# A decoder layer's self-attention with transposed scores and softmax sums from a column of ones, and the layer norms' epsilon added on POOL

## The chip, the cores and the metric

The kernel runs on one core of a Trainium2 chip. The metric is the device time of one execution in microseconds (us); smaller is better. Five engines work side by side, each through its own instructions in order, and wait for one another by semaphores: TensorE (PE; its weight loads are listed as PEld), VectorE (DVE), ScalarE (ACT), GpSimd (POOL) and SyncE (SP, which issues DMAs). PE's results lie in PSUM, which the code declares as eight banks of 128 partitions by 512 fp32 columns.

## The reference, cut to what matters

4096 tokens (64 sequences of 64) of width 128 pass through a self-attention, a cross-attention and a mixture of experts, each followed by a residual sum and a layer norm. The change lies in the self-attention (16 heads of 64, one shared key and value head) and in the layer norms of both attentions:

```python
def layernorm(x, g):
    mean = jnp.mean(x, axis=-1, keepdims=True)
    var = jnp.var(x, axis=-1, keepdims=True)
    return (x - mean) * jax.lax.rsqrt(var + EPS) * g
...
xn = layernorm(x, g1)
q = xn @ Wq.T
kv = xn @ Wkv.T
k, v = (kv[..., :DIM_HEAD], kv[..., DIM_HEAD:])
...
q, k = (l2norm(q), l2norm(k))
q, k = (q * srt, k * srt)
sim = jnp.einsum('bhid,bjd->bhij', q, k)
sim = jnp.where(causal_mask, max_neg, sim)
attn = jax.nn.softmax(sim.astype(jnp.float32), axis=-1).astype(sim.dtype)
out = jnp.einsum('bhij,bjd->bhid', attn, v)
out = out.transpose(0, 2, 1, 3).reshape(b, n, HEADS * DIM_HEAD)
out = out @ Wout.T
return layernorm(out, g2)
...
x = _layernorm(x + _L0_attn_ref(x, ...), axis=-1)
```

## The kernel before

The tokens are 32 tiles of 128 (two sequences each). The kernel first passes all tiles through the self-attention, then all through the cross-attention, then through the experts. Everything is written by hand: for each engine a function `body(i, p)` lists the stages of pass i, and `stage_of(fn, i, p, back)` calls a stage for tile i - back, so that one pass works on the layer norm of tile i + 2, the projections of tile i, the scores of i - 1, the values of i - 2, the output projection of i - 3 and the second norm of i - 4. Each engine goes through its stages in the order of that list; `wait_ge` on a semaphore holds the engine there. `pipeline` writes passes 0 to 7 out, runs the middle ones as a hardware loop of two passes, and writes the last ones out; the last stages of the last tiles run inside the first cross-attention passes (`cross(0)`, `cross(1)`).

A tile goes through the self-attention like this.

- DVE takes the statistics of a row (`ln_stats`, `ln_var`) and adds epsilon to the variance; POOL raises that to the power -0.5 (`ln_in`); DVE normalises (`ln_b`); PE transposes (`x_T`, line 1526); ACT and DVE split the result in two parts.
- PE multiplies by Wq in three passes for each 512 columns (lines 1515 to 1517, banks 2 and 3) and by Wkv (line 1539, bank 1).
- ACT squares (`squares`); DVE sums over each head (`sums`, line 974: 16 heads and the key, 17 sums from 1088 columns); POOL raises all 17 to the power -0.5 in one instruction (`norms`, line 534, tile `rq`); DVE caps them (`rinv`, line 981) and scales q out of PSUM in two halves (`qn`, line 987). PE can overwrite bank 2 or 3 with the next tile's q once its half is scaled.
- PE transposes q and k (lines 1548, 1554), adds the causal mask (line 1564) and multiplies (`scores`, line 1569): 32 products of 64 x 64 x 64, each recorded as two passes, for two sequences and two groups of heads, so that queries lie on partitions. ACT takes the exponential (`exp_half`).
- DVE sums over the keys (`softmax`, lines 1003 and 1005: `L`, `rL`); POOL multiplies the 1024 columns by the reciprocals (`weights`, line 539, tile `PR`).
- PE transposes the weights (`p_T`, line 1583), ACT copies them out (line 726), PE multiplies with a block-diagonal copy of v (`values`, line 1591; DVE and ACT write that copy, lines 997 and 710), ACT copies out (`o_T`, line 734), PE projects (`project`, line 1599).
- The second and third layer norm of the tile follow on DVE (`y_stats` to `tail_c`), with two more powers on POOL (`y_rstd`, line 544, and `z_rstd`, line 548).

In the profile `bank` is a PSUM bank, `arena` holds `wide`, `qn`, `OT` and Wout, `PT` the transposed weights, `VBD` the block-diagonal v.

Of the kernel before, what the change touches and what calls it, by code (L numbers as in the profile page):

```python
# [31 lines left out]
P = 128  # L32
# [16 lines left out]
def decoder(nc, x, ctxT, g1, wqT, wkvT, woutT, g2, xwq, xwk, xwvT, xwo, bo, wrT, br, wl1, bl1, wl2, bl2, bN, out, xbuf, zbuf):  # L49
# [24 lines left out]
    HVO = HEADS // NVO  # L74

    ctx = ExitStack()
    with ctx:
# [6 lines left out]
        bank = [ctx.enter_context(nc.psum_tensor(f"bank{i}", [P, 512], F32)) for i in range(8)]  # L84
# [6 lines left out]
        mhalf = sb("mhalf", [P, 32])  # L91
        euler = sb("euler", [P, 32])
# [12 lines left out]
        OT = arena[:, 2 * W:3 * W].rearrange("p (a q) -> p a q", a=NBLK)  # L105
# [30 lines left out]
        vS = sb("vS", [P, 2, DH])  # L136
# [13 lines left out]
        rL = sb("rL", [P, 2, HEADS])  # L150
        mx = sb("mx", [P, HEADS])
# [81 lines left out]
        zeroed, w_ids = sem("zeroed"), sem("w_ids")  # L233
# [11 lines left out]
        def staging(n):  # L245
# [11 lines left out]
            "pT_ps", "pT", "y", "r", "rb", "z1", "zrstd", "x2")}  # L257
# [14 lines left out]
        def pipeline(eng, body, first, last):  # L272


            for i in range(first):
                body(i, i % 2)
            with eng.Fori(first // 2, T // 2 - 1) as j:
                body(2 * j, 0)
                body(2 * j + 1, 1)
            for i in range(T - 2, last + 1):  # L280
                body(i, i % 2)
# [192 lines left out]
        def _(pool):  # L474
            def ln_in(t, p):
                pool.wait_ge(a["stats"], 3 * t + 3)
                nc.gpsimd.tensor_tensor(rs[:, p, :], ve[:, p, :], mhalf[:, 0:1], ALU.pow).then_inc(a["rstd"], 1)
# [6 lines left out]
            nc.gpsimd.memset(euler[:, :], 2.718281828459045).then_inc(consts, 1)  # L484
# [57 lines left out]
            def y_rstd(t, p):  # L542
                pool.wait_ge(a["y1"], 3 * t + 3)
                nc.gpsimd.tensor_tensor(rs2[:, :], ve2[:, :], mhalf[:, 0:1], ALU.pow).then_inc(a["yrstd"], 1)

            def z_rstd(t, p):
                pool.wait_ge(a["z1"], 3 * t + 3)
                nc.gpsimd.tensor_tensor(rs3[:, :], ve3[:, :], mhalf[:, 0:1], ALU.pow).then_inc(a["zrstd"], 1)  # L548
# [8 lines left out]
            def body(i, p):  # L557
# [3 lines left out]
                stage_of(norms, i, p, 0)  # L561
                stage_of(z_rstd, i, p, 4)
                stage_of(ln_in, i, p, -2)
                stage_of(y_rstd, i, p, 3)
                stage_of(weights, i, p, 1)
# [8 lines left out]
            def cross_tail(t, p):  # L574
                pool.wait_ge(b["z1"], 3 * t + 3)
                nc.gpsimd.tensor_tensor(rs3[:, :], ve3[:, :], mhalf[:, 0:1], ALU.pow).then_inc(b["zrstd"], 1)  # L576
# [81 lines left out]
        def _(act):  # L658

            def x_T(t, p):  # L660
                act.wait_ge(a["xT_ps"], t + 1)
                if later(t, 2):
                    act.wait_ge(a["q"], 2 * (t - 1))
                    act.wait_ge(a["xlo"], t - 1)
                nc.scalar.activation(xT[:, p, :], bank[first_x_bank(t)][:, 0:P], ACT.Copy, scale=g1_sb[:, 0:1])\
# [8 lines left out]
            def squares(t, p):  # L674
                if later(t, 1):
                    act.wait_ge(a["ssq"], t)
                for c in range(2):
                    act.wait_ge(a["q"], 2 * t + c + 1)
                    nc.scalar.activation(wide[:, c * HW:(c + 1) * HW], bank[2 + c][:, :], ACT.Square)\
                      .then_inc(a["sq"], 1)  # L680
                act.wait_ge(a["kv"], t + 1)
                nc.scalar.activation(wide[:, W:W + DH], bank[1][:, 0:DH], ACT.Square).then_inc(a["sq"], 1)
                if later(t, 2):
                    act.wait_ge(a["v0"], t - 1)
                    act.wait_ge(a["v1"], t - 1)
                nc.scalar.activation(vS[:, p, :], bank[1][:, DH:2 * DH], ACT.Copy).then_inc(a["vS"], 1)
# [1234 lines left out]
```

## Time and profile before

| what | before |
|---|---|
| time, median of 3 runs | 832.95 us (831.18 to 836.39) |
| the profiled execution | 833.86 us, its span 832.1 us |
| busy over the span | PE 770.5 us (93%), DVE 620.7 (75%), ACT 596.5 (72%), POOL 454.3 (55%) |
| self-attention | until some 330 us; cross-attention follows until some 690 us, then the experts |
| granted PE clock | 0.987 of full speed on the mean |

Times are from the start of the span. Busy shares are means over stages with different limits, and a busy PE is not PE at its peak, since its instructions overlap in the record. What bounds a stage is read from the waits and from the order in time within that stage.

### The profile page before, as it was taken

How to read it: one execution, taken by the hardware profiler on the slowest of the kernel's cores; microseconds unless marked ns; L12 is line 12 of the kernel's file. 1: busy time of each engine (PE TensorE's matmuls, PEld its weight loads, DVE VectorE, ACT ScalarE, POOL GpSimd, SP SyncE). 2: the span in 40 equal slices, each digit the busy share in tenths (PEclk: the TensorE clock that was granted, in tenths of full speed). 3: DMA queues.
4: the chain of work that ended last, by engine and by line, in shares of the span. 5: the costliest groups of instructions: out<-in, count | busy, mean ns of one | idle time of the engine just before them, and what ended most of it. 6: DMA issues, size and time to landing. Idle time of an engine off the chain costs nothing.

```text
span 832.1 us, 26529 instructions
## 1 busy us (share of the span) xinstructions
PE 770.5 (93%) x9276; PEld 646.4 (78%) x9308; DVE 620.7 (75%) x1834; ACT 596.5 (72%) x1444; POOL 454.3 (55%) x442
## 2 busy tenths in 40 slices
PE   3799999999999998899899999999999989989995
PEld 3577778777777877788788888887888878989962
DVE  3877878878877874789888888888888965744425
ACT  2688888878878874777778777676767667767735
POOL 6467776776777672222253535444443537776643
PEclk9899999999999999999999999999999989999998
DMA  8299999100000000000000000000000227878745
GB/s 273 67 159 165 162 161 156 16 0 0 0 0 0 0 3 2 6 7 7 7 22 17 23 17 20 20 20 20 16 23 14 72 76 225 254 221 250 248 157 210
DMA packets 69392, 64.79 MB, mean 78 GB/s; under 512 B 5702, under 2 KB 54985, under 8 KB 69168
## 3 DMA queue, kind: packets, MB, share of 16 engines
q1 hardware_dynamic: 62592, 51.42, 29.8%
q0 software_dynamic: 4624, 9.61, 3.3%
q10 hardware_dynamic: 2080, 2.49, 1.0%
q8 instruction: 59, 0.97, 0.5%
q14 instruction: 37, 0.30, 0.1%
HBM read 35.37 MB, written 28.58 MB: 77 GB/s over the span
## 4 chain that ended last, share of the span: by engine, by line
PE 47%; issue 19%; POOL 13%; DVE 9%; ACT 6%; DMA 3%; SPq 1%; POOLq 0%; DVEq 0%; ACTq 0%
PE bank L1715 7%; PE bank L1819 6%; PE bank L1515 5%; POOL rq L534 5%; PE bank L1517 5%; PE bank L1516 5%; POOL PR L539 3%; PE bank L1829 3%; PE bank L1703 3%; PE bank L1591 2%; PE bank L1599 2%; PE bank L1690 2%; ACT VBD L393 2%; DMA w_now<-in_wl 2%; POOL rs L548 1%
## 5 line engine op out<-in xcount | busy, mean ns | idle before, releaser
L393 ACT COPY VBD<-bank 64x512 f32<-64x512 f32 x192 | 111.4, 580 | 28.1 <-PE bank L1517 25.4
L571 POOL TENSOR_TENSOR PR<-PR,rL 128x1024 f32<-128x1024 f32 x32 | 60.9, 1904 | 107.9 <-DVE rL L1125 107.7
L534 POOL TENSOR_TENSOR rq<-ssq,mhalf 128x17 f32<-128x17 f32 x32 | 99.3, 3102 | 14.4 <-DVE ssq L974 13.8
L539 POOL TENSOR_TENSOR PR<-PR,rL 128x1024 f32<-128x1024 f32 x32 | 61.0, 1905 | 82.4 <-DVE rL L1005 82.4
L638 POOL DMA_INDIRECT zbuf<-arena x71 | 69.8, 983 | 31.6 <-issue 21.2
L626 POOL DMA_INDIRECT xbuf<-xg,slot x64 | 64.9, 1013 | 34.2 <-DVE xg L1320 21.6
L1819 PE MATMUL bank<-xT,w_now 128*128 128x128 f32 x568 | 77.3, 280 | 3.1 <-DMA w_now<-in_wl 2.7
L1819 PEld LDWEIGHTS bank<-xT,w_now 128*128 128x128 f32 x568 | 70.4, 195 | 4.6 <-issue 3.5
L1446 DVE SCALAR_TENSOR_TENSOR stage<-bank,b_now,early 128x128 f32<-128x128 f32 x142 | 43.3, 347 | 40.4 <-ACT early L892 32.6
L892 ACT ACTIVATE early<-bank,b_now 128x128 f32<-128x128 f32 x142 | 44.6, 365 | 35.8 <-PE bank L1819 35.7
L1715 PE MATMUL bank<-VBD,PT 128*64 128x128 f32 x1024 | 64.7, 280 | 3.2 <-ACT PT L808 3.2
L1715 PEld LDWEIGHTS bank<-VBD,PT 128*64 128x64 f32 x1024 | 56.8, 139 | 11.8 <-ACT PT L808 9.8
L1599 PE MATMUL bank<-arena 128*128 128x128 f32 x512 | 63.0, 276 | 1.1 <-ACT arena L734 0.7
L1591 PE MATMUL bank<-PT,VBD 128*128 128x512 f32 x128 | 63.4, 617 | 0.0
L808 ACT ACTIVATE PT<-bank 128x512 f32<-128x512 f32 x64 | 38.3, 600 | 34.7 <-PE bank L1703 34.0
L1599 PEld LDWEIGHTS bank<-arena 128*128 128x128 f32 x512 | 59.8, 192 | 2.3 <-ACT arena L734 1.6
L576 POOL TENSOR_TENSOR rs<-ve,mhalf 128x1 f32<-128x1 f32 x32 | 18.6, 581 | 70.5 <-DVE ve L1140 70.2
L1515 PE MATMUL bank<-vo_lo,cT_hi 96*128 96x512 f32 x128 | 54.8, 428 | 2.3 <-DVE VBD L393 1.5
L1112 DVE TENSOR_REDUCE mx<-bank 128x8 f32<-128x512 f32 x64 | 43.8, 684 | 17.3 <-PE bank L1690 17.0
L718 ACT ACTIVATE PR<-bank 128x512 f32<-128x512 f32 x64 | 34.7, 595 | 28.8 <-PE bank L1569 28.8
L1517 PE MATMUL bank<-vo_hi,cT_hi 96*128 96x512 f32 x128 | 50.4, 394 | 0.0
L1516 PE MATMUL bank<-vo_hi,cT_lo 96*128 96x512 f32 x128 | 50.4, 394 | 0.0
(253 smaller groups left out, 2296.0 us busy)
## 6 DMA issues: line engine op xcount, KB each, us to landing
w_now<-in_wl SPq DMA_DIRECT2D x71, 256.0 KB
xbuf<-blank SPq DMA_DIRECT2D x1, 17160.0 KB, 119.6
arena<-xbuf SPq DMA_DIRECT2D x71, 65.0 KB
VBD<-zbuf SPq DMA_DIRECT2D x4, 512.0 KB, 5.0
out<-X SPq DMA_DIRECT2D x8, 256.0 KB, 2.3
cT<-in_ctxT ACTq DMA_DIRECT2D x16, 96.0 KB, 1.9
zbuf<-arena POOLq DMA_INDIRECT x71
wl_sb<-in_wl POOLq DMA_DIRECT2D x1, 1024.0 KB, 8.5
```

What stands on the lines that cost most here:

```text
L393: u = copy(VBD[h * SEQ:(h + 1) * SEQ, p, s, lo:lo + blocks, :], bank[CHUNK_BANK[c]][s * SEQ:(s + 1) * SEQ, :].rearrange("k (a d) -> k a d" ...
L534: nc.gpsimd.tensor_tensor(rq[:, :], ssq[:, :], mhalf[:, 0:HEADS + 1], ALU.pow).then_inc(a["pow"], 1)
L539: nc.gpsimd.tensor_tensor(v, v, rL[:, p, :].unsqueeze(2).broadcast_to([P, HEADS, SEQ]), ALU.mult)\
L626: nc.gpsimd.indirect_dma_start(out=xbuf, out_offset=at, in_=xg[:, k, tt, :], in_offset=None)\
L638: nc.gpsimd.indirect_dma_start(out=zbuf, out_offset=at, in_=yb[:, t % YB, :], in_offset=None, bounds_check=K2 * TOK - 1, oob_is_err=False) ...
L1515: M(out_, l_hi, r_lo, start=True, stop=False)
L1516: M(out_, l_lo, r_hi, start=False, stop=False)
L1517: return M(out_, l_hi, r_hi, start=False, stop=True)
L1591: M(bank[4 + s][:, :], VBD[:, p, s, 0, :], PT[:, s * HW:(s + 1) * HW], start=True, stop=True)\
L1599: m = M(bank[0][:, 0:D], OT[:, k, :], wout_sb[:, k, :], start=(k == 0), stop=(k == NBLK - 1))
L1715: m = M(bank[bk][s * SEQ:(s + 1) * SEQ, 0:D], PT[:, k * P + s * SEQ:k * P + (s + 1) * SEQ], VBD[:, p, s, k, :], start=(k == 0), stop=(k == ...
L1819: m = M(bank[2 + q % 2][:, c * P:(c + 1) * P], w_now[:, q, c * P:(c + 1) * P], xT[:, q % 2, :], start=True, stop=True)
```

## The change

Three things change.

The **attention** is turned round. The scores are computed with keys on partitions (`scores`: kT is the stationary operand, four products of 64 x 64 x 512 take the place of 32 products of 64 x 64 x 64, and the mask is transposed too). Their exponential is then already the stationary operand of the product with v, so the transpose of the weights (`p_T`), its copy, and the block-diagonal v go away. v has a column of ones behind it (`kvS`, 129 columns, kept for four tiles), so that each of 32 products of 64 x 64 x 65 (`values`) gives 64 output columns and the softmax sum. DVE takes the reciprocal of the 16 sums from PSUM and scales the output while it copies it out (`o_norm`: two reciprocals, a product of 128 columns and two of 448); the sum over keys on DVE and the multiplication of the weights on POOL go away. PE transposes the scaled output (`o_T`, eight transposes), ACT copies it, and `project` has 16 products of 128 x 64 instead of eight of 128 x 128. PSUM is one tensor, `psum`.

The **norm of q** is cut in two halves: squares, sums (8 and 9), powers (8 and 9 columns), caps and scaling each run in two instructions, so that the first half does not wait for the second.

The **epsilon** of the layer norms of both attentions is added on POOL: `rsqrt` there is an addition, a wait for it, and the power. The additions on DVE go away.

The stages stand in a new order on DVE, ACT and PE, and the hardware loop has four passes (`VB = 4`). The memory for the block-diagonal v is no longer cleared at the start.

```diff
+        def rsqrt(dst, ve, var, done, t):
+            nc.gpsimd.tensor_tensor(ve, var, epsilon[:, :], ALU.add).then_inc(done, 1)
+            pool.wait_ge(done, t + 1)
+            return nc.gpsimd.tensor_tensor(dst, ve, mhalf[:, 0:1], ALU.pow)
...
             def norms(t, p):
-                pool.wait_ge(a["ssq"], t + 1)
-                if later(t, 1):
-                    pool.wait_ge(a["cap"], t)
-                nc.gpsimd.tensor_tensor(rq[:, :], ssq[:, :], mhalf[:, 0:HEADS + 1], ALU.pow).then_inc(a["pow"], 1)
-
-            def weights(t, p):
-                pool.wait_ge(a["sum"], 2 * t + 2)
-                v = PR[:, p, :].rearrange("q (h k) -> q h k", k=SEQ)
-                nc.gpsimd.tensor_tensor(v, v, rL[:, p, :].unsqueeze(2).broadcast_to([P, HEADS, SEQ]), ALU.mult)\
-                  .then_inc(a["norm"], 1)
+                for c in range(2):
+                    s = half(c)
+                    pool.wait_ge(a["ssq"], 2 * t + c + 1)
+                    if later(t, 1):
+                        pool.wait_ge(a["cap"], 2 * (t - 1) + c + 1)
+                    nc.gpsimd.tensor_tensor(rq[:, s], ssq[:, s], mhalf[:, s], ALU.pow).then_inc(a["pow"], 1)
...
+            def o_norm(t, p):
+                dve.wait_ge(a["o"], t + 1)
+                first = psum[:, 4:6, 0:O_LAST * O_W].rearrange("q s (a d) -> q s a d", d=O_W)
+                last = psum[:, 0:2, O_AT:O_AT + O_W]
+                V.reciprocal(rO[:, :, O_LAST:NBLK], last[:, :, DH:O_W]).then_inc(a["rO"], 1)
+                V.reciprocal(rO[:, :, 0:O_LAST], first[:, :, :, DH]).then_inc(a["rO"], 1)
+                if later(t, 1):
+                    dve.wait_ge(a["oT_ps"], 2 * t)
+                dve.wait_ge(a["rO"], 2 * t + 1)
+                V.tensor_tensor(On[:, :, O_LAST, :], last[:, :, 0:DH],
+                                rO[:, :, O_LAST:NBLK].broadcast_to([P, PB, DH]), ALU.mult).then_inc(a["on"], 1)
+                dve.wait_ge(a["rO"], 2 * t + 2)
+                for s in range(PB):
+                    V.tensor_tensor(On[:, s, 0:O_LAST, :], first[:, s, :, 0:DH],
+                                    rO[:, s, 0:O_LAST].unsqueeze(2).broadcast_to([P, O_LAST, DH]), ALU.mult)\
+                     .then_inc(a["on"], 1)
...
-                for k in range(NBLK):
+                for s in range(PB):
+                    q = slice(s * SEQ, (s + 1) * SEQ)
                     for h in range(2):
                         r = slice(h * DH, (h + 1) * DH)
-                        for s in range(PB):
-                            m = M(bank[6 + h][s * SEQ:(s + 1) * SEQ, k * SEQ:(k + 1) * SEQ],
-                                  QT[r, p, k, s * SEQ:(s + 1) * SEQ], kT[r, p, s * SEQ:(s + 1) * SEQ],
-                                  start=False, stop=(k == NBLK - 1))
-                        if k == NBLK - 1:
+                        m = M(bank[6 + h][q, :], kT[r, p, q], QT[r, p, :, q], start=False, stop=True)
+                        if s == PB - 1:
                             m.then_inc(a["s"], 1)
...
-                stage_of(qkv, i, p, 0)
+                self_stage(q_product, i, p, 0)
+                self_stage(lambda t, q: o_T(t, q, 0), i, p, 3)
+                self_stage(lambda t, q: o_T(t, q, 1), i, p, 3)
+                self_stage(kv_product, i, p, 0)
...
-                stage_of(qk_T, i, p, 1)
-                stage_of(x_T, i, p, -1)
-                stage_of(project, i, p, 3)
-                stage_of(lambda t, q: p_T(t, q, 0), i, p, 2)
-                stage_of(lambda t, q: p_T(t, q, 1), i, p, 2)
-                stage_of(scores, i, p, 1)
-                stage_of(lambda t, q: values(t, q, 0), i, p, 2)
-                stage_of(lambda t, q: values(t, q, 1), i, p, 2)
+                self_stage(qk_T, i, p, 1)
+                self_stage(x_T, i, p, -1)
+                self_stage(project, i, p, 3)
+                self_stage(scores, i, p, 1)
+                self_stage(values, i, p, 2, True)
```

DVE, one tile of the self-attention, before (from the cap of the norms on; `L` and `rL` are the softmax sums and reciprocals):

```order
L981 TENSOR_TENSOR rinv<-rq,caps 128x17
L987 TENSOR_TENSOR arena<-bank,rinv 128x512 x2
L1046 TENSOR_SCALAR X<-r,mv,rs 128x128
L962 TENSOR_SCALAR xn<-X,mv,rs 128x128
L997 COPY VBD<-vS 64x64 x2
L1003 TENSOR_REDUCE L<-PR 128x16
L1005 RECIPROCAL rL<-L 128x16
L943 BN_STATS st<-X 128x6
L974 TENSOR_REDUCE ssq<-arena 128x17
```

DVE, the same place now (line numbers are those of the changed kernel; `rO` holds the reciprocals, `PT` now the scaled output, and 128x8 and 128x9 are the two halves of the sums):

```order
L971 TENSOR_SCALAR xn<-X,mv,rs 128x128
L1030 BN_AGGR mv<-st 128x2
L1034 SCALAR_TENSOR_TENSOR yg<-yS,mv,g_sb 128x128
L1007 RECIPROCAL rO<-psum 128x2
L1008 RECIPROCAL rO<-psum 128x2x7
L1012 TENSOR_TENSOR PT<-psum,rO 128x2x64
L1016 TENSOR_TENSOR PT<-psum,rO 128x448 x2
L984 TENSOR_REDUCE ssq<-arena 128x8
L954 BN_STATS st<-X 128x6
L1042 SCALAR_TENSOR_TENSOR r<-yg,rs,X 128x128
L1048 BN_STATS st<-r 128x6
L984 TENSOR_REDUCE ssq<-arena 128x9
```

The scaling of the output stands between the first norm of a later tile (`xn`) and the sums of the squares, and the statistics of the third norm (`r`, `st`) stand ahead of the second half of those sums.

POOL, one tile, before (`PR` are the softmax weights, `rq` the 17 norms, `rs` the third, first and second layer norm in this order):

```order
L539 TENSOR_TENSOR PR<-PR,rL 128x1024
L534 TENSOR_TENSOR rq<-ssq,mhalf 128x17
L548 TENSOR_TENSOR rs<-ve,mhalf 128x1
L477 TENSOR_TENSOR rs<-ve,mhalf 128x1
L544 TENSOR_TENSOR rs<-ve,mhalf 128x1
```

POOL, one tile now (each `ve` is a variance with epsilon added):

```order
L572 TENSOR_TENSOR rq<-ssq,mhalf 128x8
L572 TENSOR_TENSOR rq<-ssq,mhalf 128x9
L505 TENSOR_TENSOR ve<-mv,epsilon 128x1
L507 TENSOR_TENSOR rs<-ve,mhalf 128x1
L505 TENSOR_TENSOR ve<-mv,epsilon 128x1
L507 TENSOR_TENSOR rs<-ve,mhalf 128x1
L505 TENSOR_TENSOR ve<-mv,epsilon 128x1
L507 TENSOR_TENSOR rs<-ve,mhalf 128x1
```

The product of 1024 columns is gone, the norms are two instructions, and an addition stands ahead of each layer norm's power.

PE, one tile now, from the transposes of q and k on (before, the rows after the transpose of `xn` were eight products of 128x128, eight transposes of `PR`, the mask, 32 products of 64x64 and two of 128x512):

```order
L1620 MATMUL psum<-ident,PT 128x128 x8
L1561 MATMUL psum<-wkv_sb,xT 128x128
L1570 MATMUL psum<-ident,arena 128x128 x8
L1575 MATMUL psum<-ident,kn 128x128
L1541 MATMUL psum<-ident,xn 128x128
L1631 MATMUL psum<-arena 64x128 x16
L1586 MATMUL psum<-causal,ident_b 128x512 x2
L1591 MATMUL psum<-QT,kT 64x512 x4
```

The transposes of the output stand between the products with Wq and Wkv; 32 products of 64x65 with `kvS` follow the last row shown.

## Rows read from the trace of the kernel before

**Rows 1.** Windows, tiles 3 to 31: busy time of each engine, granted clock, DMA share

```profile
46.70:301.80 255.10, 251.23 (x3116) 199.61 (x3143) 202.66 (x607) 207.81 (x531) 182.84 (x142) 1.00 0.50 64
```

**Rows 2.** Waits in that stretch: total us, times, longest

```profile
POOL PR L539 <- DVE rL L1005: 73.5, 29, 3.2
DVE rinv L981 <- POOL rq L534: 29.9, 28, 1.5
```

**Rows 3.** Timeline, POOL and DVE, one tile: start, us, instruction

```profile
128.91 3.07 POOL L534 TENSOR_TENSOR rq<-ssq,mhalf 128x17 f32<-128x17 f32 x1
...
131.95 0.54 POOL L548 TENSOR_TENSOR rs<-ve,mhalf 128x1 f32<-128x1 f32 x1
...
132.01 0.18 DVE L981 TENSOR_TENSOR rinv<-rq,caps 128x17 f32<-128x17 f32 x1 [0.85 <-POOL rq L534]
132.31 1.29 DVE L987 TENSOR_TENSOR arena<-bank,rinv 128x512 f32<-128x512 f32 x2
...
132.46 0.55 POOL L477 TENSOR_TENSOR rs<-ve,mhalf 128x1 f32<-128x1 f32 x1
...
133.77 0.34 DVE L962 TENSOR_SCALAR xn<-X,mv,rs 128x128 f32 x1
...
134.03 0.38 DVE L997 COPY VBD<-vS 64x64 f32<-64x64 f32 x2
...
134.44 1.22 DVE L1003 TENSOR_REDUCE L<-PR 128x16 f32<-128x1024 f32 x1
...
135.69 0.25 DVE L1005 RECIPROCAL rL<-L 128x16 f32<-128x16 f32 x1
...
136.03 1.90 POOL L539 TENSOR_TENSOR PR<-PR,rL 128x1024 f32<-128x1024 f32 x1 [2.51 <-DVE rL L1005]
136.15 1.29 DVE L974 TENSOR_REDUCE ssq<-arena 128x17 f32<-128x1088 f32 x1
...
137.89 3.17 POOL L534 TENSOR_TENSOR rq<-ssq,mhalf 128x17 f32<-128x17 f32 x1
```

**Rows 4.** Timeline, POOL: the norms of tiles 3 and 31

```profile
46.74 3.07 POOL L534 TENSOR_TENSOR rq<-ssq,mhalf 128x17 f32<-128x17 f32 x1
...
301.76 3.06 POOL L534 TENSOR_TENSOR rq<-ssq,mhalf 128x17 f32<-128x17 f32 x1
```

**Rows 5.** Timeline, PE and its weight loads (PEld), same tile

```profile
128.90 0.85 PEld L1583 LDWEIGHTS bank<-ident,PR 128*128 128x128 f32 x8 [0.24 <-POOL PR L539]
...
129.72 0.21 PEld L1564 LDWEIGHTS bank<-causal,ident_b 128*128 128x128 bf16 x2
...
130.35 1.02 PEld L1569 LDWEIGHTS bank<-kT,QT 64*64 64x64 f32 x64 [0.42 <-issue]
...
131.45 1.98 PE L1591 MATMUL bank<-PT,VBD 128*128 128x512 f32 x4
...
133.27 0.19 PEld L1516 LDWEIGHTS bank<-wq_hi,xT_lo 128*128 128x128 f32 x1
...
135.97 1.95 PE L1599 MATMUL bank<-arena 128*128 128x128 f32 x16
...
137.98 0.14 PEld L1583 LDWEIGHTS bank<-ident,PR 128*128 128x128 f32 x1 [0.25 <-POOL PR L539]
```

**Rows 6.** Groups by line: count, busy us, mean ns

```profile
L654 POOL TENSOR_TENSOR frs<-fve,mhalf 128x4 f32<-128x4 f32 x8 | 8.1, 1013 | 13.5 <-DVE fve L1495 13.5
...
L363 POOL TENSOR_TENSOR xs<-X,ones 128x128 f32<-128x128 f32 x32 | 12.3, 408 | 0.2
...
L1042 DVE TENSOR_SCALAR ve<-mv 128x1 f32<-128x1 f32 x32 | 4.9, 154 | 0.0
```

**Rows 7.** Timeline, POOL, start of the kernel: the second instruction waits for the first

```profile
1.75 0.10 POOL L486 MEMSET caps<- 128x1 f32 x1
1.93 0.29 POOL L488 TENSOR_SCALAR_AFFINE_SELECT ident<-ident 128x128 f32<-128x128 f32 x1
```

**Rows 8.** Windows, ten short DVE instructions in a row

```profile
128.94:131.15 2.21, 2.16 (x61) 1.77 (x66) 1.92 (x10) 1.36 (x3) 2.21 (x1) 1.00 1.27 162
```

**Rows 9.** Timeline, weight loads of a cross-attention tile: 16 products of 128x64, then 128x128

```profile
412.92 1.73 PEld L1715 LDWEIGHTS bank<-VBD,PT 128*64 128x64 f32 x32
414.81 0.10 PEld L1743 LDWEIGHTS bank<-picked,tri_b 128*128 128x128 bf16 x1 [0.17 <-issue]
```

**Rows 10.** Page, groups: the cross-attention's layer norm power on POOL

```profile
L576 POOL TENSOR_TENSOR rs<-ve,mhalf 128x1 f32<-128x1 f32 x32 | 18.6, 581 | 70.5 <-DVE ve L1140 70.2
```

More of the change, by code:

```diff
@@ L275, in pipeline @@
             for i in range(first):
[L276 to L281, printed above, removed]
+                body(i, i % VB)
+            with eng.Fori(first // VB, T // VB - 1) as j:
+                for k in range(VB):
+                    body(VB * j + k, k)
+            for i in range(T - VB, last + 1):
+                body(i, i % VB)
         A_FIRST = 8
@@ L399, in has, with half, self_stage @@
             return 0 <= t < T if isinstance(t, int) else True
+        def half(c):
+            return slice(c * HEADS // 2, (c + 1) * HEADS // 2 + c)
+        def self_stage(fn, i, p, back, deep=False):
+            t = i - back
+            if isinstance(t, int) and not 0 <= t < T:
+                return
+            q = t % VB if isinstance(t, int) else (p - back) % VB
+            fn(t, q if deep else q % 2)
         def stage_of(fn, i, p, back):
@@ L560, in body @@
                     fetch(1, 1)
[L561 to L565, printed above, removed]
+                self_stage(norms, i, p, 0)
+                self_stage(z_rstd, i, p, 4)
+                self_stage(ln_in, i, p, -2)
+                self_stage(y_rstd, i, p, 3)
             pipeline(pool, body, A_FIRST, T - 1)
@@ L925, in _ @@
             V = nc.vector
-            V.memset(VBD[:, :, :, 0, :], 0.0).then_inc(zeroed, 1)
             def split_slice(n):
@@ L992, in v_bd, with cap @@
-            def v_bd(t, p):
-                dve.wait_ge(a["vS"], t + 1)
-                if later(t, 2):
-                    dve.wait_ge(a["o"], 2 * (t - 1))
-                for h in range(2):
-                    v = V.tensor_copy(VBD[h * DH:(h + 1) * DH, p, 0, 0, h * DH:(h + 1) * DH], vS[0:SEQ, p, :])
-                v.then_inc(a["v0"], 1)
-            def softmax(t, p):
-                dve.wait_ge(a["exp"], 2 * (t + 1))
-                v = PR[:, p, :].rearrange("q (h k) -> q h k", k=SEQ)
-                V.tensor_reduce(L[:, :], v, AX.X, ALU.add).then_inc(a["sum"], 1)
-                dve.wait_ge(a["sum"], 2 * t + 1)
-                V.reciprocal(rL[:, p, :], L[:, :]).then_inc(a["sum"], 1)
+            def cap(t, p, c):
+                dve.wait_ge(a["pow"], 2 * t + c + 1)
+                if c == 1 and later(t, 1):
+                    dve.wait_ge(a["kn"], t)
+                V.tensor_tensor(rinv[:, half(c)], rq[:, half(c)], caps[:, half(c)], ALU.min).then_inc(a["cap"], 1)
@@ new lines, in values @@
+            def values(t, p):
+                if isinstance(t, int):
+                    pe.wait_ge(a["exp"], 2 * (t + 1))
+                    pe.wait_ge(a["kvS"], t + 1)
+                for k in range(NBLK):
+                    if k == O_LAST:
+                        pe.wait_ge(b["vo_lo"], NVO)
+                        if later(t, 1):
+                            pe.wait_ge(a["yS"], t if not isinstance(t, int) or t < T - 1 else T - 2)
+                        pe.wait_ge(a["xT"], upto_tile(t + 4))
+                    for s in range(PB):
+                        rows = slice(s * SEQ, (s + 1) * SEQ)
+                        for h in range(2):
+                            to = bank[s][:, O_AT:O_AT + O_W] if k == O_LAST else bank[4 + s][:, k * O_W:(k + 1) * O_W]
+                            at = h * HW + k * SEQ
+                            m = M(to[h * SEQ:(h + 1) * SEQ, :], PR[rows, p % 2, at:at + SEQ], kvS[rows, p, V_ONE],
+                                  start=True, stop=True)
+                m.then_inc(a["o"], 1)
@@ new lines, in o_T @@
+            def o_T(t, p, s):
+                pe.wait_ge(a["on"], 3 * t + 2 + s)
+                pe.wait_ge(a["exp"], 2 * upto_tile(t + 2))
+                if later(t, 1):
+                    pe.wait_ge(a["oT"], 2 * t)
+                for g in range(HBLK):
+                    m = nc.tensor.transpose(bank[6 + s][:, g * P:(g + 1) * P],
+                                            On[:, s, 2 * g:2 * g + 2, :].rearrange("q a d -> q (a d)"), ident[:, :])
+                m.then_inc(a["oT_ps"], 1)
```

322 lines of the change are left out of this document (155 added, 167 removed).

## The prediction, made before the result was known

> **What bounds the kernel now.** The change lies in the self-attention, so I read the windows and the waits of that stretch first, then one tile in order of time. The norms of tile 3 start at 46.74 us and those of tile 31 at 301.76: 28 tiles in 255.02 us, 9.11 us a tile [rows 4]. Over that stretch PE is recorded as busy for 251 of 255 us at a granted clock of 1.00, DVE, ACT and POOL for 203, 208 and 183 [rows 1]. That looks like a PE bound. The waits say otherwise: in 28 passes out of 28 DVE waits for POOL's norms, and POOL, 29 times, for DVE's reciprocals [rows 2]. Two engines that wait for each other make a loop, and the timeline of one tile closes it [rows 3]. POOL's norms start at 128.91 and DVE caps them from 132.01 (3.10 later); DVE scales q, finishes two layer norms, copies v, sums the softmax and ends the reciprocal at 135.94 (3.93); POOL starts the weights at 136.03 (0.09) and the next norms at 137.89 (1.86). Together 8.98, against 9.11 on the mean. The norms of the next tile stand behind the weights in POOL's queue, so this loop sets the pace.
>
> PE is close behind. In its row of the same tile the transposes of the weights stand still until POOL has written them (0.24 us), and 0.42 is listed as idle ahead of the scores' loads [rows 5]; part of that is the mask at work. Some 0.3 to 0.45 us of its 9.1 are gaps. So the kernel must get shorter on POOL with DVE and on PE alike, or nothing is gained.
>
> **What goes, comes and moves.** From the loop go the weights on POOL (1.90), and on DVE the sum over keys (1.22), the reciprocal (0.25) and the copy of v (0.38) [rows 3]. The cut of the norms lets the first half run ahead. What closes now is another loop, over the second half. I follow it through the orders shown with the change: second norms, the power of the third layer norm and that of the first (POOL); then `xn`, the second norm's mean and scale, the scaling of the output, the first half's sums, three short steps, the second half's sums (DVE); and the second norms again.
>
> POOL's part. A power takes 0.55 us for one column [rows 3], 1.01 for four [rows 6] and 3.07 for 17 [rows 3], which is 0.39 and 0.158 a column. Nine columns are 1.81, eight 1.65. No row has a small addition on POOL. The nearest two-input products take 0.41 for 128 columns [rows 6] and 1.90 for 1024 [rows 3], 1.66 ns a column and 0.20 at one column. Below it lies the clearing of one column, 0.10 [rows 7]; above it the power of one column, 0.55. I take 0.20, since addition and product are the same form. The wait for its own result costs 0.08 (1.85 to 1.93) [rows 7]. So a layer norm on POOL has 0.28 more. Third norm 0.28 + 0.51, from start to start, first norm 0.28 + 0.55, second norms 1.81: 3.43.
>
> DVE's part. Ten short instructions in a row, with their waits, take 2.21 us, 0.22 each [rows 8]. The new stretch has nine of them (`xn`, the mean, `yg`, two reciprocals, the 128-column product, two statistics, `r`); more of them wait for the result just ahead or for two or three semaphores, and I take 0.26, so 2.34, with 0.22 as the lower end. Two products of 448 columns go by 1.29 for two of 512 [rows 3]: 1.13. The sums of 512 and 576 columns go by 1.29 for 1088 [rows 3], with 0.08 for each start: 0.65 and 0.72. Entry, exit and the wait for the last statistic are some 0.35. Together 5.19 (4.8 with the lower end). The loop is 3.43 + 5.19 = 8.62, between 8.2 and 8.7 for these terms.
>
> PE's part. From 133.27 to 135.97 PE does q, k and v, nine transposes for q and k and that of `xn`: 2.70 [rows 5]. Added: eight transposes of the output, priced as those of the weights that go away, 0.91 (129.72 less 128.90 for eight gives 0.82 for their loads). The projection takes the form of the cross-attention's second product, 1.73 for 16 of 128 x 64 [rows 9], for 1.86 (135.97 to 137.83). The mask stays at 0.5 to 0.63. The values take the form of the old scores, 64 passes in 1.02 [rows 5], with 65 columns for 64: 1.04, in place of 1.82 (131.45 to 133.27). The wide scores are not shown anywhere. A pass of 512 columns over the whole array takes 0.43 (four passes, 1.98, start at that spacing) [rows 5]. The old scores' 64 passes of 64 columns would take 64 x 0.43 / 8 = 3.4 one after the other and took 1.02, so 3.3 of four tiles ran abreast. The same work in four products is then 0.86 to 1.02; I take 0.92, and all in a row would be 3.44. The shape of PE's tile changes twice more in a tile; the gaps at such places are 0.07 to 0.17 [rows 5, 9], so 0.26. Together 2.70 + 0.91 + 1.73 + 0.55 + 1.04 + 0.92 + 0.26 = 8.11, and with up to 0.4 of waits for the scaling of the output and for k, 8.1 to 8.5.
>
> A page of the Trainium skill speaks against the two extra changes of shape: by "TensorEngine Tiling (Array Packing)", Tiling Modes, Key Properties, a change of tiling mode drains TensorE. The gap of 0.17 ahead of the first whole-array load behind 128 x 64 tiles agrees with a short drain [rows 9], and at that price for all four changes in a tile PE's sum would be 8.5, still under the other loop.
>
> ACT loses two copies of 512 columns and the copies of v, and is not near. So the pace is that of POOL with DVE, and I take 8.65: 0.46 a tile, 28 x 0.46 = 12.9. The first two tiles pay for POOL's additions in the open, 2 x 0.28 = 0.6. The clearing of `VBD` that goes is hidden under the load of X, so it gives nothing. In the cross-attention the addition moves from DVE (0.15 [rows 6]) to POOL (0.28); POOL sits idle there 70.5 us until the variance comes [rows 10], and behind the instruction in its queue are the sends to the experts and the softmax weights of another tile, which have that slack; I count nothing, and 32 x 0.13 = 4 if that cover is gone. At the hand-over two tiles' scaling and transposes stand in a row where the transposes and copies of the weights stood; I count 0 and keep 1.5 on both sides. The extra code of the longer loop I count at nothing, as the stretch written out runs at the same pace (46.74 on) as the loop. The profiled execution took 833.86 (span 832.1); 833.86 - 12.9 + 0.6 = 821.6. The median is 0.9 lower, so **821 us**. A measurement of this kernel can tell about 1% from no change.
>
> **The rivals.** (1) *The addition on POOL costs as much as a power.* Then two more times 0.35 stand in the loop, 9.32 a tile, 28 x 0.21 + 1.4 = 7 slower: 840. It decides from 0.45 an addition with its wait of 0.08 on. For it: the fixed part of a power is 0.39. Against it: the two products' rows. The Trainium skill's "GPSIMD Engine Reference", Engine selection, says that a two-input elementwise operation belongs on VectorE and is about twice as slow on GpSimd. Twice 0.154 would be 0.31 in place of 0.20, and would leave 827; no run here shows such an addition. (2) *The wide scores do not run four abreast.* Two abreast make 1.72 and PE's loop 8.9 to 9.3, about 833; one after the other 3.44, PE's loop 10.7 to 11, and some 45 to 50 us slower, 880. It turns the sign from 1.8 us on. Against it stands the old scores' row. (3) *DVE waits more than I count.* Its new order puts the scaling of the output ahead of all sums, and each 0.3 of further waits in the loop gives back 8 us: 829 to 833, no change. (4) *Loop and PE both at their lower ends* (0.10 for an addition, 0.22 for a short step): 8.25 a tile, 28 x 0.86 = 24 faster, 810. That the weights' product or the sum over keys does not go is excluded by the orders.
>
> **How the numbers follow.** Forecast (815 to 826) 0.42; (3) 0.21; (4) 0.14; (1) 0.10; (2) two abreast 0.07, in a row 0.04; 0.02 for what I don't see. Nine tenths of the forecast and all of (4) lie below 824.6, 1% under 832.95: faster 0.52. Slower by over 1%, above 841.3, are the scores in a row, half of (1) and a third of two abreast and the rest: 0.14. Within 1%: 0.34. The range reaches over (4) to (1): 808 to 841; what is left out is the scores in a row and the tails of (1) and (4).
>
> **What would show it.** In the changed profile: powers of 8 and 9 columns at 1.65 and 1.81; additions at 0.20 with 0.08 behind; the four wide scores within 1.0 us; the norms of a tile every 8.6 to 8.7 us; DVE waiting for the first norm's power ahead of `xn`, and POOL for the second sums. I am wrong if PE's mask or the products behind it wait for the scores (then 2), if the additions take over 0.45 (1), or if the pace is right and the cross-attention gives it back.

## The result and the profile after

The changed kernel takes 838.74 us (median of 10 runs, 836.33 to 841.58), the kernel before 832.07 beside it (10 runs, 830.11 to 836.39): a ratio of 1.008, with a 95% interval of 1.0063 to 1.0097. I had predicted 821. The profiled execution took 838.47, its span is 836.7 us, 4.6 more than before.

The start of PE's first product with Wq in tiles 3, 12 and 31, and of the first scores of the cross-attention, cut the span into stretches. From the timeline of the weight loads (start, us, instruction, idle time ahead of it and its releaser), before:

```profile
42.23 0.19 PEld L1515 LDWEIGHTS bank<-wq_lo,xT_hi 128*128 128x128 f32 x1 [2.37 <-issue]
...
123.97 0.19 PEld L1515 LDWEIGHTS bank<-wq_lo,xT_hi 128*128 128x128 f32 x1 [0.46 <-DVE arena L987]
...
296.48 0.19 PEld L1515 LDWEIGHTS bank<-wq_lo,xT_hi 128*128 128x128 f32 x1 [0.38 <-issue]
...
329.87 1.02 PEld L1690 LDWEIGHTS bank<-KT,QT 64*64 64x64 f32 x64
```

The same places after:

```profile
36.12 0.19 PEld L1532 LDWEIGHTS psum<-wq_lo,xT_hi 128*128 128x128 f32 x1
...
136.31 0.19 PEld L1532 LDWEIGHTS psum<-wq_lo,xT_hi 128*128 128x128 f32 x1 [0.43 <-issue]
...
299.86 0.19 PEld L1532 LDWEIGHTS psum<-wq_lo,xT_hi 128*128 128x128 f32 x1
...
335.44 1.02 PEld L1722 LDWEIGHTS psum<-KT,QT 64*64 64x64 f32 x64 [0.17 <-issue]
```

| stretch | before | after | difference |
|---|---|---|---|
| up to tile 3 | 42.23 | 36.12 | -6.1 |
| tiles 3 to 12 | 81.74 | 100.19 | +18.5 |
| tiles 12 to 31 | 172.51 | 163.55 | -9.0 |
| tile 31 to the first cross scores | 33.39 | 35.58 | +2.2 |
| the rest | 502.2 | 501.3 | -1.0 |

Tiles 12 to 31 run at 8.61 us each, as forecast. Nine tiles at the beginning eat all of it: 100.19 us where nine times 8.61 would be 77.5, so 22.7 too much. The windows of tiles 3 to 13 and 13 to 31 (by the starts of the norms; busy time of PE, its loads, DVE, ACT and POOL, then granted clock, DMA share, GB/s) show that in the first stretch no engine is as busy as later; PE is recorded as busy for 85% of it against 98% behind it:

```profile
38.73:147.27 108.54, 92.27 (x1322) 70.34 (x1321) 69.07 (x217) 59.23 (x151) 56.00 (x78) 0.94 1.23 153
147.27:302.31 155.04, 152.67 (x2379) 117.37 (x2378) 125.82 (x394) 105.01 (x271) 102.19 (x145) 1.00 0.00 1
```

Before, tiles 3 to 13 went at the pace of all others (46.74 to 137.89, [rows 3, 4]) although the DMA engines were as busy. The timeline of PE's loads in the first stretch, reduced to the stops of over 1.2 us, has them in the middle of groups of like products, where PE waits for no other engine:

```profile
43.59 0.63 PEld L1631 LDWEIGHTS psum<-arena 128*64 128x64 f32 x10 [2.05 <-issue]
...
53.50 1.17 PEld L1631 LDWEIGHTS psum<-arena 128*64 128x64 f32 x21 [1.88 <-issue]
...
63.57 1.73 PEld L1631 LDWEIGHTS psum<-arena 128*64 128x64 f32 x32 [1.80 <-issue]
...
73.37 1.36 PEld L1570 LDWEIGHTS psum<-ident,arena 128*128 128x128 f32 x7 [2.04 <-issue]
...
83.19 0.64 PEld L1620 LDWEIGHTS psum<-ident,PT 128*128 128x128 f32 x6 [1.31 <-issue]
...
94.42 0.28 PEld L1610 LDWEIGHTS psum<-kvS,PR 64*64 64x64 f32 x2 [4.51 <-issue]
...
116.28 0.55 PEld L1610 LDWEIGHTS psum<-kvS,PR 64*64 64x64 f32 x29 [2.45 <-issue]
```

They add up to 16.0 us. The loads counted from one stop to the next are 121, 121, 123, 123, 122 and 237, at whatever product that falls, and the first six stops lie 10.2 us apart on the mean. So something comes in portions of some 122 loads with their 122 products. The DMA queues have it: the page counts 65 transfers on q8, of the kind "instruction", with 1.06 MB, 16 KB each. In 40 to 147 us (queue, kind: packets, MB, share):

```profile
q1 hardware_dynamic: 31242, 16.24, 121.9%
q8 instruction: 11, 0.18, 0.8%
```

The stops follow these transfers. Each of the seven has the start of one q8 transfer in the stretch from 3.15 to 2.55 us ahead of its end, though such transfers come only about every 10 us. For the stop of 4.51 us that stretch is 91.27 to 91.87:

```profile
q8 instruction: 1, 0.02, 12.6%
```

In 160 to 280 us, inside the hardware loop, nothing is fetched:

```profile
DMA packets 0, 0.00 MB, mean 0 GB/s; under 512 B 0, under 2 KB 0, under 8 KB 0
```

The 16.24 MB on q1 are, but for 16 KB, the clearing of `xbuf`, a transfer of 17 MB that takes 119.6 us. SP starts it at 31.26 us here and at 36.88 before, and not at 20 us, as the expectations below have it. So the theory: PE's code for the passes written out and for the first round of the loop is loaded while the clearing fills the DMA engines, one block (one 16 KB transfer) per 10.2 us. PE after the change needs 132.1 loads a tile (2378 over 18 tiles) and uses a block up in 122 / 132.1 x 8.61 = 8.0 us; before, with 112.3 loads (3143 over 28 tiles [rows 1]) it took 9.9 us, about as long as one takes to come. The Trainium skill, "Runtime: NRT & Kernel Launch", Instruction fetch mechanics, says that the sequencer refills its instruction memory in blocks of 16 KiB, 256 instructions, and that the crossing of a block is mostly hidden. The 16 KB and the 242 to 246 loads and products per stop agree with the first; under the clearing the crossing is not hidden.

The steady tile, as PE's loads (one tile of those behind 147 us):

```profile
183.59 1.73 PEld L1631 LDWEIGHTS psum<-arena 128*64 128x64 f32 x32
185.49 0.11 PEld L1586 LDWEIGHTS psum<-causal,ident_b 128*128 128x128 bf16 x2 [0.17 <-issue]
186.03 0.21 PEld L1591 LDWEIGHTS psum<-QT,kT 64*64 64x64 f32 x8 [0.42 <-issue]
...
186.94 0.97 PEld L1610 LDWEIGHTS psum<-kvS,PR 64*64 64x64 f32 x60 [0.28 <-issue]
187.98 0.19 PEld L1532 LDWEIGHTS psum<-wq_lo,xT_hi 128*128 128x128 f32 x1
...
189.27 1.01 PEld L1620 LDWEIGHTS psum<-ident,PT 128*128 128x128 f32 x8
190.24 0.30 PEld L1561 LDWEIGHTS psum<-wkv_sb,xT 128*128 128x128 f32 x2
```

And POOL in the same tile:

```profile
181.86 1.65 POOL L572 TENSOR_TENSOR rq<-ssq,mhalf 128x8 f32<-128x8 f32 x1 [1.65 <-DVE ssq L984]
183.72 1.80 POOL L572 TENSOR_TENSOR rq<-ssq,mhalf 128x9 f32<-128x9 f32 x1 [0.21 <-DVE ssq L984]
185.49 0.19 POOL L505 TENSOR_TENSOR ve<-mv,epsilon 128x1 f32<-128x1 f32 x1
185.76 0.56 POOL L507 TENSOR_TENSOR rs<-ve,mhalf 128x1 f32<-128x1 f32 x1
...
187.71 0.19 POOL L505 TENSOR_TENSOR ve<-mv,epsilon 128x1 f32<-128x1 f32 x1 [0.55 <-DVE mv L1030]
```

PE goes from group to group with only short gaps, and does not wait for DVE's scaled output ahead of its transposes (189.27). POOL and DVE wait more. That is another picture than my loop of POOL and DVE, with the same pace.

### The profile page after: what moved, and what is told of

Same layout as the page of the kernel before. It is cut to its first block, busy times and chain, and to the rows that moved or that the text cites. A ratio compares the mean times of both kernels' runs of the same rounds, so it can differ in the third digit from the quotient of the medians.

```text
span 836.7 us, 27882 instructions
## 1 busy us (share of the span) xinstructions
PE 761.3 (91%) x9948; PEld 631.6 (75%) x9948; DVE 603.9 (72%) x1801; ACT 546.7 (65%) x1316; POOL 431.9 (52%) x572
## 3 DMA queue, kind: packets, MB, share of 16 engines
q8 instruction: 65, 1.06, 0.6%
## 4 chain that ended last, share of the span: by engine, by line
PE 61%; DVE 15%; issue 10%; ACT 7%; DMA 4%; SPq 1%; POOL 0%; DVEq 0%; ACTq 0%; POOLq 0%
PE psum L1631 7%; PE psum L1853 6%; PE psum L1747 6%; PE psum L1532 5%; PE psum L1534 4%; PE psum L1533 4%; PE psum L1591 4%; PE psum L1610 4%; PE psum L1620 4%; PE psum L1570 3%; DVE VBD L409 3%; PE psum L1863 3%; ACT VBD L409 2%; DVE mx L1129 2%; PE psum L1586 2%
## 5 line engine op out<-in xcount | busy, mean ns | idle before, releaser
L572 POOL TENSOR_TENSOR rq<-ssq,mhalf 128x8 f32<-128x8 f32 x64 | 111.1, 1737 | 87.8 <-DVE ssq L984 87.6
L409 ACT COPY VBD<-psum 64x512 f32<-64x512 f32 x192 | 111.2, 579 | 28.0 <-PE psum L1534 25.3
L602 POOL TENSOR_TENSOR PR<-PR,rL 128x1024 f32<-128x1024 f32 x32 | 60.9, 1902 | 103.3 <-DVE rL L1142 103.1
L1853 PE MATMUL psum<-xT,w_now 128*128 128x128 f32 x568 | 76.7, 278 | 3.0 <-DMA w_now<-in_wl 2.5
L1853 PEld LDWEIGHTS psum<-xT,w_now 128*128 128x128 f32 x568 | 69.8, 193 | 4.3 <-issue 3.6
L1631 PE MATMUL psum<-arena 128*64 128x128 f32 x1024 | 64.7, 279 | 6.7 <-issue 5.1
L1747 PE MATMUL psum<-VBD,PT 128*64 128x128 f32 x1024 | 64.7, 280 | 3.2 <-ACT PT L821 3.2
L1747 PEld LDWEIGHTS psum<-VBD,PT 128*64 128x64 f32 x1024 | 56.8, 139 | 12.1 <-ACT PT L821 10.2
L1631 PEld LDWEIGHTS psum<-arena 128*64 128x64 f32 x1024 | 56.5, 139 | 11.8 <-issue 6.6
L1532 PE MATMUL psum<-vo_lo,cT_hi 96*128 96x512 f32 x128 | 54.9, 429 | 1.8 <-DVE VBD L409 1.5
## 6 DMA issues: line engine op xcount, KB each, us to landing
xbuf<-blank SPq DMA_DIRECT2D x1, 17160.0 KB, 119.6
```

The costliest lines, as they stand in the source:

```text
L409: u = copy(VBD[h * SEQ:(h + 1) * SEQ, p, s, lo:lo + blocks, :], bank[CHUNK_BANK[c]][s * SEQ:(s + 1) * SEQ, :].rearrange("k (a d) -> k a d" ...
L572: nc.gpsimd.tensor_tensor(rq[:, s], ssq[:, s], mhalf[:, s], ALU.pow).then_inc(a["pow"], 1)
L1532: M(out_, l_hi, r_lo, start=True, stop=False)
L1631: m = M(bank[y_bank(t)][s * SEQ:(s + 1) * SEQ, 0:D], OT[:, s, g, c, :], wout_sb[:, c * HBLK + g, :], start=(c == 0 and g == 0), stop=(c == ...
L1747: m = M(bank[bk][s * SEQ:(s + 1) * SEQ, 0:D], PT[:, k * P + s * SEQ:k * P + (s + 1) * SEQ], VBD[:, p, s, k, :], start=(k == 0), stop=(k == ...
L1853: m = M(bank[2 + q % 2][:, c * P:(c + 1) * P], w_now[:, q, c * P:(c + 1) * P], xT[:, q % 2, :], start=True, stop=True)
```

## The experiments

**Is it the code under the clearing?** The clearing is only started later. In the changed kernel until the sums of tile 12 (e1) or of tile 28 (e4, 58 in place of 26), in the kernel before until those of tile 12 (e2, 13 in place of 26):

```diff
             sp.wait_ge(consts, CONSTS)
+            sp.wait_ge(a["ssq"], 26)
             sp.dma_start(xbuf.rearrange("(p a) d -> p a d", p=P),
```

> The changed kernel, but SP starts the clearing of xbuf (17 MB, 119.6 us) only when the sums of tile 12 are done, not at 20 us. Code theory: PE stands still at 44 to 147 us because its next block of instructions is late while the clearing fills the DMA engines; in the trace these stops lie some 122 weight loads apart. Without the clearing there they go: no idle of PE over 1 us put down to issue between 40 and 147 us, norms every 8.6 us from tile 4 on, tile 13's at 124 to 128 us instead of 147.27, and 814 to 821 us in all. Order theory (the new order of the stages fills slowly, or the first tiles wait for one another): the stops stay, 836 to 841. Middle: if the loading is slow even without the clearing, the stops shrink and the time lies between 822 and 835.

Measured: 818.2 us, 0.9824 of the kernel before (0.9789 to 0.9859). The stops are gone (no idle time over 1 us is put down to issue from 40 to 147 us): tiles 3 to 12 take 77.2 us (38.35 to 115.55) in place of 100.19, and the norms of tile 13 start at 127.18. The code theory holds, and the change is a gain with a late clearing.

> The kernel before with the same delay of the clearing (until the sums of tile 12). Its PE has some 112 weight loads a tile of 9.11 us, so a block of 122 lasts 9.9 us, about what comes in while the clearing runs, and its trace shows no such stops. Code theory: nothing to gain, 829 to 833. Rival (the clearing slows the engines or memories in general): faster here too, by as much as in the changed kernel.

833.37 us, 0.9992 (0.9965 to 1.0019). The clearing costs the kernel before nothing that can be told; it is not the memories in general. The 2.37 us put down to issue ahead of tile 3 before (42.23) stay here too, so those don't come from the clearing.

> The changed kernel, with the clearing started when the sums of tile 28 are done (some 255 to 280 us), so that it ends before the first sends to the experts near 410 us. Code theory: the stops of 44 to 147 us go as with the other delay (some 20 us), and new stops of PE come where the written-out passes and the cross-attention load their code under the clearing, between 260 and 400 us: 818 to 833 us, slower than the earlier start by 3 to 15 us. Order theory: stops at 44 to 147 us as before, 836 to 841.

838.11 us, 1.0033 (1.0005 to 1.006), beyond my 833. Tiles 3 to 12 are clean (36.37 to 113.90), and the stops have moved with the clearing, to where the last passes and the cross-attention are loaded:

```profile
284.79 1.29 PEld L1632 LDWEIGHTS psum<-arena 128*64 128x64 f32 x23 [1.82 <-issue]
...
295.49 1.50 PEld L1632 LDWEIGHTS psum<-arena 128*64 128x64 f32 x26 [1.70 <-issue]
...
305.85 0.19 PEld L1534 LDWEIGHTS psum<-cT_hi,xwk_lo 96*128 96x128 f32 x1 [2.24 <-issue]
...
320.89 0.24 PEld L1632 LDWEIGHTS psum<-arena 128*64 128x64 f32 x4 [4.01 <-issue]
```

Between the first two lie 122 loads and 10.7 us, much as in the changed kernel. The stops of tiles 3 to 12 thus come from the clearing, and not from the order or shape of those tiles. Not all of the 20 us beyond e1 is late code: the first four loads of the cross-attention's context land after 6.2 us in the median, against 2.0 for all 16, and PE waits for that, which it doesn't in e1:

```profile
342.85 0.51 ACT L797 ACTIVATE cT_hi<-cT 96x128 fp32r<-96x128 f32 x2 [3.75 <-DMA cT<-in_ctxT]
...
344.58 0.19 PEld L1533 LDWEIGHTS psum<-cT_lo,xwk_hi 96*128 96x128 f32 x1 [1.89 <-DVE cT_lo L1123]
```

**The longer loop alone** (e3), in the kernel before:

```diff
-            with eng.Fori(first // 2, T // 2 - 1) as j:
-                body(2 * j, 0)
-                body(2 * j + 1, 1)
-            for i in range(T - 2, last + 1):
+            with eng.Fori(first // 4, T // 4 - 1) as j:
+                for k in range(4):
+                    body(4 * j + k, k % 2)
+            for i in range(T - 4, last + 1):
```

> The kernel before with its hardware loop of four passes in place of two; nothing else. Two more passes are loaded while the clearing runs and two more are written out at the end. Code theory: the demand per us stays as before, so 831 to 835. Rival (the longer loop alone costs the time): 836 to 840.

834.05 us, 1.0021 (0.9994 to 1.0048): the longer loop by itself costs nothing that can be told. What is left is PE's higher demand for code, which comes next.

**Demand alone** (e11), in the kernel before, and the same with the late clearing (e12):

```diff
+                            cut = 2 if k < 4 else 1
+                            n = SEQ // cut
+                            for e in range(cut):
-                            m = M(bank[6 + h][s * SEQ:(s + 1) * SEQ, k * SEQ:(k + 1) * SEQ],
+                                m = M(bank[6 + h][s * SEQ:(s + 1) * SEQ, k * SEQ + e * n:k * SEQ + (e + 1) * n],
```

> The kernel before with half of its score products cut in two along the keys (64 x 64 x 32): 32 more weight loads a tile, the same numbers computed, the clearing at 20 us as before. If a block of some 122 loads takes about 10.2 us to come while the clearing runs (the distance of the stops in the changed kernel), PE here uses one up in 122 / 144 of some 9.4 us, 8.0, and stops some 2 us at each: 15 to 28 us slower than the run with the same products and the late clearing, with stops over 1 us at 40 to 140 us. If the stops are peculiar to the changed order: the two runs are alike within 3 us.

> The same with the clearing started when the sums of tile 12 are done. It prices the added loads themselves: 0.2 to 0.5 us a tile of PE, 836 to 848, without stops over 1 us at 40 to 110 us.

856.34 us (1.0269, 1.0218 to 1.0319) and 841.61 (1.0079, 1.0046 to 1.0113): 14.7 us between them, just under the 15 to 28 that I expected. Tiles 3 to 13 take 110.8 us against 93.1 (norms from 46.71 to 157.46, and from 46.52 to 139.64). The longest stops of e11, which e12 doesn't have:

```profile
67.28 0.42 PEld L1548 LDWEIGHTS bank<-ident,arena 128*128 128x128 f32 x4 [3.06 <-issue]
...
77.26 0.29 PEld L1572 LDWEIGHTS bank<-kT,QT 64*64 64x64 f32 x4 [4.58 <-issue]
...
91.78 0.54 PEld L1572 LDWEIGHTS bank<-kT,QT 64*64 64x64 f32 x26 [2.81 <-issue]
```

Two more, at 57.08 and 121.65 us, are of 1.1 and 1.2 us. The first two lie 10.0 us and 124 loads apart. So the kernel before stood just inside the limit, and 32 more weight loads a tile push it over, without any of the change.

**What sets the steady pace?** All on top of the late clearing of e1. e5 adds the epsilon twice:

```diff
-                nc.gpsimd.tensor_tensor(ve, var, epsilon[:, :], ALU.add).then_inc(done, 1)
-                pool.wait_ge(done, t + 1)
+                n = 2 if done in (a["ve"], a["ve2"], a["ve3"]) else 1
+                for k in range(n):
+                    nc.gpsimd.tensor_tensor(ve, var, epsilon[:, :], ALU.add).then_inc(done, 1)
+                    pool.wait_ge(done, n * t + k + 1)
```

> The changed kernel with the late clearing (the run of 818.2 us), and each epsilon of the self-attention's layer norms added twice on POOL (the second addition writes the same number), each with its wait: 0.27 us more for each of two norms in the loop of POOL and DVE. Loop theory (as predicted: POOL and DVE set 8.6 us a tile): 0.54 more a tile, 28 tiles, 832 to 834. PE theory (PE has no gaps but those of its changes of shape and sets the pace; the loop waits 0.26 us a tile for the squares of k): only what goes over that slack counts, 8.85 a tile, 825 to 828.

828.52 us (0.995, 0.9929 to 0.997). The norms of tiles 4 to 31 start 9.00 us apart (e1: 8.62): of 0.54 us added to the loop 0.38 arrive, between the two theories (the time lies 0.5 above the range of the second). PE now waits for DVE's scaled output (waits of 60 to 270 us: total us, times, longest), for which e1 lists 1.6 us in 4 waits over the same time:

```profile
PEld psum L1623 <- DVE PT L1019: 11.5, 18, 0.8
```

e7 leaves out one of two groups of heads in `project`:

```diff
-                for c in range(2):
+                for c in range(1):
...
-                                  start=(c == 0 and g == 0), stop=(c == 1 and g == HBLK - 1))
+                                  start=(c == 0 and g == 0), stop=(g == HBLK - 1))
```

> The changed kernel with the late clearing, and the output projection of the self-attention with half of its 16 products (one of the two groups of heads is left out of the sum), which takes 0.86 us a tile from PE and nothing from the other engines. PE theory: the pace falls until the loop of POOL and DVE binds at 8.3, so 0.26 a tile and some 7 us, 808 to 813. Loop theory: no change, 816 to 820.

807.44 us (0.9715, 0.9673 to 0.9757), just under the 808 expected, norms 8.45 apart; the rest of the gain lies ahead of and behind these tiles. Again PE waits for DVE:

```profile
PEld psum L1621 <- DVE PT L1017: 20.0, 20, 1.4
```

The two agree: with PE shortened the loop of POOL and DVE takes 8.45, and 8.45 + 0.54 = 8.99 is e5's pace. So, as far as these two runs show, PE sets 8.6 unedited and the loop stands 0.17 behind it; traces of the same unedited loop differ by 0.07 (8.61 in the changed kernel behind tile 13, 8.68 in e10). The loop isn't POOL and DVE alone: in every tile DVE waits some 0.25 us for ACT's squares of k (6.4 us in 25 waits in e7).

e6 puts the epsilon back on DVE, behind each variance, four times like this; POOL then has only the power:

```diff
                 V.bn_aggr(mv3[:, :], st3[:, :]).then_inc(a["z1"], 1)
+                dve.wait_ge(a["z1"], 2 * t + 2)
+                V.tensor_scalar(ve3[:, :], mv3[:, 1:2], EPS, None, ALU.add).then_inc(a["ve3"], 1)
```

> The changed kernel with the late clearing, and every epsilon of both attentions added on DVE again, behind the variance, so that POOL has only the powers. PE theory: no change, 816 to 821. Loop theory: POOL's part is 0.54 shorter, DVE's 0.3 to 0.45 longer, 0.1 to 0.25 a tile gained, 811 to 816; if DVE's waits weigh more, 820 to 824. Cross-attention: no change by either.

818.55 us (0.9829, 0.9788 to 0.987): no change beside e1. e9 makes the opposite edit in the kernel before: the self-attention's `rsqrt` on POOL as in the change's diff, and DVE's additions go.

> The kernel before with the self-attention's three epsilons added on POOL (the cross-attention's stays on DVE). In the trace of before the DVE additions lie ahead of the wait for the norms (0.85 us idle there), and POOL has 2.5 us idle ahead of the weights, where the new additions (0.27 each) fit. Slack theory: no change, 830 to 835. Rival (the additions lengthen POOL's way to the first norm's power, for which DVE waits): 0.1 to 0.3 a tile, 835 to 842.

835.31 us (1.0023, 0.9997 to 1.0049): none that can be told, though the median is 0.3 above the 835 of the slack theory. The third part of the change, for itself, moves nothing in either kernel that these runs can tell.

e8 takes the cut of the norms back on POOL:

```diff
-                for c in range(2):
-                    s = half(c)
-                    pool.wait_ge(a["ssq"], 2 * t + c + 1)
...
-                    nc.gpsimd.tensor_tensor(rq[:, s], ssq[:, s], mhalf[:, s], ALU.pow).then_inc(a["pow"], 1)
+                pool.wait_ge(a["ssq"], 2 * t + 2)
...
+                nc.gpsimd.tensor_tensor(rq[:, :], ssq[:, :], mhalf[:, 0:HEADS + 1], ALU.pow).then_inc(a["pow"], 2)
```

> The changed kernel with the late clearing, and POOL's norms in one power of 17 columns behind both halves of the sums, as in the kernel before; all else stays. If the cut is what lets the rest gain: the loop is 1.3 us longer, 9.3 to 9.8 a tile, 840 to 855. If PE sets the pace and the cut brings little: 818 to 826.

867.99 us (1.0425, 1.0383 to 1.0466), 10.25 a tile: more than I expected, since both halves of q now also wait for the whole power. DVE's caps wait for it:

```profile
DVE rinv L990 <- POOL rq L571: 62.2, 20, 3.2
```

With this order of the stages, the turned attention without the cut is slower than the kernel before.

**The hand-over** (e10), with the late clearing:

```diff
-                    values(T - 1, (T - 1) % VB)
-                    for t in (T - 2, T - 1):
-                        for s in range(PB):
-                            o_T(t, t % 2, s)
-                        project(t, t % 2)
+                    for s in range(PB):
+                        o_T(T - 2, (T - 2) % 2, s)
+                    values(T - 1, (T - 1) % VB)
+                    project(T - 2, (T - 2) % 2)
+                    for s in range(PB):
+                        o_T(T - 1, (T - 1) % 2, s)
+                    project(T - 1, (T - 1) % 2)
```

> The changed kernel with the late clearing, and at the hand-over the output of tile 30 transposed ahead of the values of tile 31, so that ACT's copy (1.04 us in which PE stands) runs beside those values. One wait of 1.04 goes: 816 to 818 against 818.2. If the next stage waits for something else anyway: no change.

815.95 us, 0.9788 of the kernel before (0.973 to 0.9846), the fastest that leaves nothing out; its interval and e1's overlap. The traces tell them apart: tile 31's first product with Wq starts at 279.65 in e1 and 279.66 here, the first cross scores at 315.19 and 312.72, so 2.5 us earlier, more than the one wait of 1.04 expected.

## Why the prediction was wrong

The step that failed is the sentence "The extra code of the longer loop I count at nothing, as the stretch written out runs at the same pace (46.74 on) as the loop". The same pace showed that the kernel before had its code in time, not by how much. There was in effect no margin: before, seven q8 transfers start within 59 us (49.7 to 108.8), 9.85 us apart on the mean, and PE took 9.9 to use a block up. The change raises PE's loads from 112 to 132 a tile, shortens the tile and has 11 blocks come under the clearing in place of these 7. That cost 22.7 us in the trace, and 20.5 between the medians of the changed kernel and e1. Of the 22.7, 16.0 are the stops listed. For the rest there is the clock, which was lower where PE stood still: 0.91, 0.83, 0.93 and 0.98 of full speed in the four stretches of 20 us from 60 to 140 us, 1.00 in e1. My estimate from these four is 0.35 x 20 = 7.0 us, for 6.7 left. The late code was in no term and in no rival, though the page of before lists 59 instruction transfers on q8, and the windows a DMA share above 1 [rows 8] over the very passes whose code was being loaded.

The rest, by the steps:

- *The pace.* 8.65 forecast, 8.61 measured; 28 tiles are worth 28 x (9.08 - 8.61) = 13.2 (forecast 12.9; 9.08 is 254.25 / 28 before). Right in size, but by the wrong engine, and in that a matter of luck: the loop of POOL and DVE is 8.45 (8.62 forecast), PE 8.6, a little above the upper end of my 8.1 to 8.5.
- *POOL.* Powers of 8 and 9 columns 1.65 and 1.80 (1.65 and 1.81), an addition 0.19 with 0.08 behind it (0.20 and 0.08). Rival 1 is out, and so is the 0.31 that I worked out from the Trainium skill's "GPSIMD Engine Reference", Engine selection: at one column POOL takes 0.19 for DVE's 0.15 [rows 6], whose addition has one input and a constant.
- *PE's new forms.* The wide scores take 0.91 (186.03 to 186.94; 0.92 forecast), so four abreast; the values 1.04 (1.04). Rival 2 is out. PE's sum was short by some 0.5. A row misread is 0.21 of it: 133.27 [rows 5] is the second of the six products with Wq, and the first starts at 133.06, so that stretch took 2.91 and not 2.70. The rest is waits and gaps around the transposes of k and `xn` and the projection. Rival 3 would have to show as a longer loop, and it is shorter.
- *The prologue.* +0.6 forecast, -6.1 measured (-3.9 in e1, -5.9 in e4). I counted two additions and not that a tile's chain is shorter when no weights wait for sums. That this is the cause was not tried.
- *The hand-over.* 0 +- 1.5 forecast, +2.2 measured; e10 brings 2.5 back.
- *Cross-attention and experts.* 0 forecast, -1.0 measured. POOL's additions there stand behind idle time as counted.

Together -6.1 + 22.7 - 13.2 + 2.2 - 1.0 = 4.6, the difference of the spans. Without the stretch that waited for code it would have been -18; e1 has -15.6 (832.1 to 816.5), mostly because its prologue is 2.2 us longer.

## What to carry to other kernels

Code is a transfer too. Where a change raises the instructions per microsecond of one engine, or writes more passes out, look up which bulk transfer runs while that code is loaded, and start that transfer once the hardware loop turns, early enough that it ends before the next passes written out: e4, which started it late, took as long as the changed kernel. An even pace says that a resource is not short yet, not how much is left: work out supply and demand, here a block's time to arrive against the time to use it up.

## What was not expected of the hardware

Stops of one engine in the middle of a group of like instructions, with no semaphore named, at nearly equal counts of instructions (121 to 124 loads and their products), were late code here. In the three runs with the clearing over such loading the stops lie some 10 us apart (10.2 on the mean in the changed kernel, 10.7 and 10.0 between the first two shown of e4 and e11). With the clearing elsewhere the same kernels showed no such stop in the same passes. A loop of four passes (some 530 loads) is not fetched again on its later rounds: 160 to 280 us shows no transfer at all. After a stop PE's clock can fall: in 80 to 100 us, which has the two stops of 1.31 and 4.51 us, the mean granted clock is 0.83, so part of it ran at the lower level of 1.2 GHz, where before it was 1.00 (2.4 GHz). The changed kernel, then the kernel before (columns as above):

```profile
80.00:100.00 20.00, 14.47 (x172) 11.41 (x163) 10.19 (x32) 9.05 (x22) 7.94 (x10) 0.83 1.27 160
...
80.00:100.00 20.00, 19.65 (x236) 15.86 (x237) 15.63 (x47) 16.58 (x44) 13.54 (x11) 1.00 1.28 164
```
